# Batch 0 of a cross-attention and lookup-FFN layer: the sixteenth weight lookup moved between the two score stages

## The reference

```python
def _attn(q, k, v):
    s = jnp.einsum('bhqd,bhkd->bhqk', q, k) * SCALE
    p = jax.nn.softmax(s, axis=-1)
    return jnp.einsum('bhqk,bhkd->bhqd', p, v)
...
q = _ln((x @ Wq + bq).reshape(b, s1, H, HD), qn_w, qn_b)
k = _ln(kv[..., :HD], kn_w, kn_b)
ctx = _attn(qT, k.transpose(0, 2, 1, 3), v.transpose(0, 2, 1, 3))
ctx_dca = _attn(qT, k_dca.transpose(0, 2, 1, 3), v_dca.transpose(0, 2, 1, 3))
out = (ctx + ctx_dca) @ Wo + bo
...
def _ghost_linear(x, idx, lut):
    w = lut[idx]
    return jnp.einsum('bsh,oh->bso', x, w)
h = jax.nn.silu(gate) * up
...
x = x + _L0_xattn_ref(_layernorm(x, axis=-1), ctx_1024, ...)
x = x + _L0_ffn_ref(_layernorm(x, axis=-1), lut, gate_idx, up_idx, down_idx)
```

## Time and profile before

| | |
|---|---|
| time, median of 3 runs | 803.22 us (802.91 to 804.98) |
| the profiled execution's own time | 803.17 us |
| its span, first to last instruction | 801.4 us |
| granted TensorE clock, mean of the span | 0.985 |
| PE busy | 753.8 us |
| DVE, ACT, POOL busy | 502.3, 480.0, 279.2 us |
| batch 0's first score stage, on PE | from 54.9 us |
| batch 0's second score stage, on PE | 135.72 us to 201.82 us |

### The profile page before, as it was taken

How to read it: one execution, slowest core, us unless ns; L and a number is a source line. 1 busy time by engine, 2 the same in 40 slices (tenths; PEclk the granted TensorE clock), 3 DMA queues, 4 the chain that set the end, 5 groups by cost and what they waited for, 6 DMA issues and landing times.

```text
span 801.4 us, 14897 instructions
## 1 busy us (share of the span) xinstructions
PE 753.8 (94%) x5881; PEld 308.2 (38%) x5881; DVE 502.3 (63%) x966; ACT 480.0 (60%) x976; POOL 279.2 (35%) x283
## 2 busy tenths in 40 slices
PE   2887895999999999999999999999999999999998
PEld 1342231333443333324543332235433333265445
DVE  8979999577777994225879953228599810153221
ACT  3579887577456896662658866635489856511100
POOL 4996433002663322113843321035622310014320
PEclk9998998899999999999999999999999999999999
DMA  8639997577330001321400003223000000100001
GB/s 253 173 104 281 290 287 218 144 195 143 103 86 2 1 1 30 77 53 60 113 16 1 1 14 79 55 66 53 3 1 1 1 27 28 37 18 1 1 13 40
DMA packets 75909, 61.49 MB, mean 77 GB/s; under 512 B 34944, under 2 KB 62336, under 8 KB 75584
## 3 DMA queue, kind: packets, MB, share of 16 engines
q1 hardware_dynamic: 75056, 60.29, 28.3%
q10 hardware_dynamic: 784, 0.26, 0.2%
HBM read 43.55 MB, written 10.55 MB: 68 GB/s over the span
## 4 chain that ended last, share of the span: by engine, by line
PE 73%; DVE 13%; issue 5%; POOL 4%; ACT 3%; DMA 2%; SPq 0%; DVEq 0%; POOLq 0%
PE ps L1782 46%; PE ps L2169 8%; PE ps L2150 6%; PE ps L2121 5%; PE ps L1854 5%; POOL hrstd L745 2%; PE ps L2156 2%; DVE arena L1197 2%; ACT ps L1077 2%; DMA wf_lo<-in_idx 1%; PE ps L2017 1%; DVE stat L1258 1%; DVE arena L1338 1%; DVE nmax L1575 1%; DMA arena<-in_x 1%
## 5 line engine op out<-in xcount | busy, mean ns | idle before, releaser
L1782 PE MATMUL ps<-arena,wf_hi 128*128 128x512 f16 (+1 forms) x704 | 201.4, 370 | 0.8 <-DVE arena L1218 0.8
L1077 ACT ACTIVATE ps<-ps,nmax 128x496 f32<-128x496 f32 x256 | 166.3, 652 | 23.1 <-DVE nmax L1580 23.1
L1109 ACT ACTIVATE arena<-ps 128x1024 f32<-128x1024 f32 x128 | 124.1, 1021 | 89.1 <-PE ps L2156 89.1
L1782 PE MATMUL ps<-arena,wf_lo 128*128 128x512 f16 (+1 forms) x352 | 130.0, 369 | 0.0
L1782 PE MATMUL ps<-wf_hi,arena 128*128 128x512 f16 (+3 forms) x374 | 114.8, 368 | 0.6 <-DVE arena L1222 0.6
L745 POOL TENSOR_TENSOR hrstd<-hvar,mhalf 128x16 f32<-128x16 f32 (+1 forms) x33 | 100.2, 3049 | 43.4 <-DVE hvar L1328 43.3
L1782 PEld LDWEIGHTS ps<-arena,wf_hi 128*128 128x128 f16 x704 | 64.8, 98 | 83.7 <-issue 20.5
L1854 PE MATMUL ps<-arena,wf_lo 128*32 128x512 fp8e4 (+1 forms) x1056 | 65.9, 390 | 9.4 <-DVE wf_lo L1206 7.8
L689 POOL TENSOR_TENSOR xrstd<-xvar,mhalf 128x1 f32<-128x1 f32 x32 | 21.3, 666 | 151.9 <-DVE xvar L1263 151.9
L1782 PE MATMUL ps<-wf_lo,arena 128*128 128x512 f16 (+3 forms) x187 | 68.5, 366 | 0.0
L2169 PE MATMUL ps<-arena 128*32 128x512 f32 x512 | 68.3, 605 | 0.0
(11 more groups left out here) (164 smaller groups left out, 1073.5 us busy)
## 6 DMA issues: line engine op xcount, KB each, us to landing
arena<-bits SPq DMA_DIRECT2D x124, 128.0 KB, 3.8
arena<-in_x SPq DMA_DIRECT2D x32, 256.0 KB, 2.9
wf_lo<-in_idx SPq DMA_DIRECT2D x10, 512.0 KB, 5.1
bits<-wf_hi SPq DMA_DIRECT2D x10, 384.0 KB, 5.8
out<-arena SPq DMA_DIRECT2D x15, 256.0 KB, 2.1
wf_lo<-in_idx SPq DMA_DIRECT2D x11, 256.0 KB, 8.7
arena<-in_ctxT SPq DMA_DIRECT2D x5, 512.0 KB, 3.7
v_next<-arena SPq DMA_DIRECT2D x8, 256.0 KB, 6.3
```

What stands on the lines that cost most here:

```text
L1077: last = act.activation(sc, sc, ACT.Exp, bias=nmax[:, 0, t, h:h + 1], accum_out=den[:, 0, t, h:h + 1])
L1109: act.activation(probs[n_ % 2][:, 2 * p:2 * p + 2, :], ps[:, bank:bank + 2, :], ACT.Exp).then_inc(s["probs_set"], 1)
L1782: last = pe.matmul(dst, l, r, start=(first and i == 0), stop=(stop and i == len(todo) - 1))
```

## The change

Lookup 15 leaves slot 0 and is done on PE between the two score stages, ahead of the four transposes. Each slot's lookup on PE and its high part on ACT is then that of one chunk more: `look_up(16+n)` and `lookup_out(16+n)` in slot n. DVE's part of a slot keeps its numbers: `one_hot(17+n)`, `low_out(15+n)`; slot 15 gets the last `one_hot(32)`, which stood in batch 1's `core`. Of the two lookups at the start of batch 1 one is left (32, at AHEAD). The last early projection goes to a bank of the scores (TB) and no more stands in the list `SHARED`; it waits for the exponentials of step 29, and `scores_t(0)` waits for its result to be out. On ACT `lookup_out(14)` moves behind the exponentials of step 30, and the last `early_out` and `lookup_out(15)` stand behind the logarithm. On DVE `low_out(14)` and both halves of `one_hot(15)` stand ahead of the last row sum, one half of `one_hot(16)` behind it and the other behind `caugT`, and the four products that make the low halves of Wo, which stood behind `caugT`, go two by two into slots 0 and 1.

```diff
@@ SHARED, LATE
-    if EARLY_FROM <= i_ < EARLY_FROM + len(EARLY):
+    if EARLY_FROM <= i_ < EARLY_FROM + len(EARLY) - 1:
         SHARED += [("early", i_ - EARLY_FROM)]
...
-LATE = {AHEAD: NCH - 2, AHEAD + 1: NCH - 1}
+LATE = {AHEAD: NCH - 1}
...
+        early_bank = lambda e: TB if e == len(EARLY) - 1 else shared_bank("early", e)
@@ ACT, prepare
-                if S_ONE <= slot < S_SUM:
+                if S_ONE <= slot < S_SUM - 1:
                     for c in lookups_in(slot):
                         if 0 <= c - EARLY_FROM < len(EARLY):
                             early_out(c - EARLY_FROM)
-                        if c < NQ - 1:
+                        if c < NQ - 2:
                             lookup_out(c)
+                if slot == S_SUM - 2:
+                    lookup_out(NQ - 2)
+                if slot == S_SHIFT + 1:
+                    early_out(len(EARLY) - 1)
+                    lookup_out(NQ - 1)
                 if slot >= S_TWO:
                     for c in lookups_in(slot):
-                        lookup_out(c - 2)
+                        lookup_out(c - 1)
@@ DVE, batch 1's core
                     normalise(a, 1, False)
-                    one_hot(NCH - 1, (0,))
                     low_out(NCH - 2)
                     residual(0, prev)
                     moments(2, 0, prev, rows_of(0))
-                    one_hot(NCH - 1, (1,))
@@ DVE, prepare
+                if slot == S_SUM:
+                    low_out(NQ - 2)
+                    one_hot(NQ - 1)
+                if slot == S_SHIFT:
+                    one_hot(NQ, (0,))
                 if slot == S_SHIFT + 1:
+                    one_hot(NQ, (1,))
+                if slot in (S_TWO, S_TWO + 1):
                     dve.wait_ge(s["wo_hi"], G)
-                    for g in range(G):
+                    for g in range(slot - S_TWO, G, 2):
                         low(wo[1][:, g, :], st_o[:, g * D:(g + 1) * D], wo[0][:, g, :]).then_inc(s["wo_lo"], 1)
-                if slot == S_SUM:
-                    one_hot(NQ - 1, (1,))
                 for c in lookups_in(slot):
-                    if c < NCH - 1:
-                        one_hot(c, (0,) if c == NQ - 1 else range(NJ))
-                    if slot < S_SUM - 1 and c:
-                        low_out(c - 1)
-                    if slot >= S_SHIFT + 1:
+                    if slot < S_SUM - 1:
+                        one_hot(c)
+                        if c:
+                            low_out(c - 1)
+                    elif slot >= S_TWO:
+                        one_hot(c)
                         low_out(c - 2)
@@ PE, early, scores_t, prepare
+                if e == len(EARLY) - 1:
+                    pe.wait_ge(s["S_exp"], NS - 2)
+                else:
+                    wait_bank("early", e)
...
+                    elif prev is None:
+                        wait_early(len(EARLY) - 1)
...
+                if slot == S_SHIFT:
+                    look_up(NQ - 1)
                 for c in lookups_in(slot):
                     if slot < S_SUM and c:
                         look_up(c - 1)
                     elif slot >= S_TWO:
-                        look_up(c - 2)
+                        look_up(c - 1)
```

More of the change, by code:

```diff
@@ L903, in early_out @@
                         act.wait_ge(s["tr_lo"], len(UNITS_0))
-                    act.activation(v_early[t], ps[:, shared_bank("early", e), :], ACT.Copy, scale=1.0 / WS).then_inc(s["v_evac"], 1)
+                    act.activation(v_early[t], ps[:, early_bank(e), :], ACT.Copy, scale=1.0 / WS).then_inc(s["v_evac"], 1)
                 else:
                     act.wait_ge(s["k_done"], e - T + 1)
-                    act.activation(k_early[t], ps[:, shared_bank("early", e), :], ACT.Copy).then_inc(s["k_evac"], 1)
+                    act.activation(k_early[t], ps[:, early_bank(e), :], ACT.Copy).then_inc(s["k_evac"], 1)
             def square(a, u, first):
@@ L1083, in core @@
                     between(S_ONE + m)
+                between(S_SUM)
                 dca_exp(a, T - 1)
@@ L1894, in early @@
                 w, c_ = (wk if kind == "k" else wv), (cT_second if kind == "w" else cT_early)
-                wait_bank("early", e)
+                if e == len(EARLY) - 1:
+                    pe.wait_ge(s["S_exp"], NS - 2)
+                else:
+                    wait_bank("early", e)
                 if e == 0:
@@ L1902, in early @@
                     terms += [(sel["k"][:, :], b16[:, :])]
-                product(ps[:, shared_bank("early", e), :], terms).then_inc(s["k_done" if kind == "k" else "v_done"], 1)
+                product(ps[:, early_bank(e), :], terms).then_inc(s["k_done" if kind == "k" else "v_done"], 1)
             def wait_early(e):
```

## The result

The changed kernel takes 820.66 us (median of 4 executions, 817.91 to 822.57) against 803.07 for the kernel before (4 executions, 801.23 to 804.98): a ratio of 1.0216, 95% interval 1.0176 to 1.0256. It is slower by 17.6 us; forecast were 822.7 and a range of 812 to 828. The profiled execution is the one of 817.91 us, span 816.1, mean clock 0.987, so what its trace accounts for is 14.7 us. The work did not change: the busy times on the page differ from the earlier trace rows by 2 us or less.

A forecast was written before the change was run, and what follows sets the result against it. PE bounds the kernel, through its idle or slow stretches in batch 0. 803.2 - 0.4 (stages) + 10.8 (slot waits) - 0.2 (slot 5) + 2.3 (batch 1) + 6.0 + 1.0 (clock) = 822.7 us, range 812 to 828.

The forecast's parts named there:

- The slots' waits: Slots 4, 8 and 12: low halves wait for low_out behind attn_lo, 3.9, 3.45 and 3.45 us, together 10.8 us lost.
- The wait at batch 1: First lookup of batch 1 (32): its low half waits for low_out(31) behind two normalisations, 2.3 us lost.
- The lookup that left batch 1: Start of batch 1: one lookup fewer on PE, counted at nothing; bound a gain of 1.9 us.
- a sign of being wrong: Batch 1: its chain getting shorter with the lookup that left it was listed as showing the prediction wrong.
- The gain between the stages: Between the score stages, to scores_t(2): gain 0.4 us; bounds a gain of 1.1 and a loss of 0.5.
- as fallen: Lookup 15 between the stages: PE's clock taken as already halved, so the lookup takes 3.61 us.
- The clock in the waits: Half-speed work after the new waits: 2.0 us for each of three slot waits, 1.0 at batch 1.
- the bound below (the clock holds): Clock loss in all four new waits: lower bound 0, upper bound 10.8 us.
- Both rows that gave the price: Earlier trace: half clock after PE waits of 1.95 and 3.02 us, read as 1.9 and 2.7 us lost.
- The rival with a clock that holds: New waits bring no clock fall: 815.7 us; chance 0.18.

The follow-up runs named there:

- slot part alone: Kernel before with only DVE's slot work put one chunk back (one_hot(16+n), low_out(14+n) in slot n): 819.55 us against 803.8, ratio 1.0202.
- second profile: Profile from running the unaltered changed kernel again: median 820.76 us against 803.5 for the kernel before, ratio 1.0203.
- waits filled: Changed kernel with PE making the high half of the lookups in slots 4, 8 and 12 four times over: 816.88 us, against 820.76 for the changed kernel.
- last version: Changed kernel with DVE also one chunk on, attn_lo behind, lookup 32 behind output rows 1, low_out ahead of the masks: 796.56 us, ratio 0.9914 to before.
- transition alone: Changed kernel between the score stages, but slots as before (lookup 15+n in slot n), lookups 31 and 32 at batch 1: 799.54 us against 803.5.

## Why the prediction was right, and where its terms were off

**The slots' waits** were the main term and came out to the hundredth: 3.91, 3.45 and 3.45 against 3.9, 3.45 and 3.45, each behind the `attn_lo` that was named. The kernel with the slot part alone shows that they need nothing else of the change, and the one with `attn_lo` moved that the order on DVE is what makes them. The rule by which they could be read off the trace of before: the result that a slot waits for is ready when its chain on DVE ends, and that moment was in the trace; only the place that asks for it moved.

**A term was left out.** A lookup that is cut in two by a wait takes longer by more than the wait: slot 12, whose clock stayed at 1.00, took 7.33 us (195.20 to 202.53), that is 3.70 + 3.45 + 0.18. The term could have been read before: slot 5 took 4.10 us there, 3.70 + 0.22 + 0.18. Four such cuts make 0.7 us.

**The wait at batch 1** was 2.26 against 2.3. **The lookup that left batch 1** was counted at nothing with a bound of 1.9; from output rows 0 to the first gate matmul it is now 25.01 us (246.69 - 221.68) against 25.34 before (231.92 - 206.58), so it gave 0.33. In the second profile it is 24.46, a gain of 0.88. So batch 1's chain did get a little shorter, which the prediction had named as a sign of being wrong; the size is under 1 us.

**The gain between the stages** was put at 0.4 and is 1.9 in the profiled execution. The sum took the clock "as fallen" for lookup 15. It ran at full clock after 3.26 us of idleness, and the execution in which it did not (with lookup 32 moved, 3.60 us) prices that step at 0.95 us. From the start of lookup 15 to `scores_t(2)` even that execution took 14.8 us where the prediction has 15.3 (148.4 - 133.1). This other 0.5 is mostly in DVE's chain, whose durations were added end to end although the rows overlap a little (138.57 + 1.41 against 139.89). The chain itself was right. The clock fell later, behind the wait of 2.35 us, and that fall cost nothing: from lookup 16's low half to `scores_t(2)` it is 6.34 us (147.29 - 140.95), and just as long in the kernel with `low_out(31)` in slot 15, whose clock stayed at 1.00 and in which PE waits for `low_out(16)` instead:

```profile
141.77 1.05 PE L1868 MATMUL ps<-arena,wf_lo 128*32 128x512 fp8e4 x16 [2.36 <-DVE wf_lo L1213]
...
147.13 1.05 PE L1868 MATMUL ps<-arena,wf_lo 128*32 128x512 fp8e4 x16 [1.48 <-DVE wf_lo L1213]
148.11 0.83 PE L2169 MATMUL ps<-arena 32*128 32x512 f16 x12
```

One count ahead of the prediction needs a correction: ahead of `shift` stand one `low_out` and half a mask more than before, not one and a half masks; three halves stand there now, and two did.

**The clock in the waits** was put at 7.0 us. In the profiled execution it fell in two of the four places and cost 0.15 + 1.43 in slots 4 and 5 (`scores_t(5)` to `scores_t(6)` takes 5.13, less 3.70) and 1.64 in slot 9: 3.2 us. Filling the three waits of the slots gave back 3.9 us by the medians and 2.95 by the profiles, where I counted 6.0 for them. So both the bound below (the clock holds) and the value taken were off, and the truth lies between. Both rows that gave the price lie behind two waits and not one: the 3.02 us stands behind the 5.38, and behind the 1.95 us PE waited again in the profile of before:

```profile
60.33 1.47 PE L2121 MATMUL ps<-arena 32*128 32x512 f16 x12 [1.54 <-ACT arena L940]
```

That may be why they priced a single wait too high; no run separates it. The Trainium skill's rule in "TensorE: Matmul & The Clock Gate", section "HAM oscillation", that a long enough wait between bursts makes the next burst start at half rate, holds in these traces often but not each time: slot 12's wait brought no fall here, and in slot 8 the low half itself still ran its 1.05 us at full clock before the fall.

The sum of the profiled execution: -1.9 between the stages, +10.8 waits, -0.4 for slot 5 (4.10 us before, 3.70 without its wait), +0.5 for the cuts, +3.2 clock, +2.4 at batch 1 with its cut, -0.3 for the lookup that left, +0.4 that the first score stage ended later: 14.7, as measured. The median is 2.75 us above this execution; the executions that make it have a lower clock, and where they lost the time no trace shows. So the forecast of 822.7 lay 2.0 above the median but 4.8 above the execution that can be followed: the clock was put 3.8 too high and the gain 1.5 too low, and the cuts that were left out took some of that back. That it came as near to the median as it did is in part luck; the waits are not. The rival with a clock that holds (815.7) is refuted by the windows and by the run with the waits filled.

**Where the expected gain of the change went:** it is there, 4.0 us when the slots keep their old numbers and 7.2 us in the last version, in which all engines are shifted. The change moved PE and ACT by one chunk and left DVE where it was, and that used up the slot of slack in which DVE's chain had run out.

## What to carry to other kernels

When work in a software pipeline is moved by one step on one engine, list every result that it consumes and look up in the trace at which moment of its own step that result is ready; the slack of a whole step can hide a chain that is as long as a step. If an engine's program order puts a cheap result that others wait for behind a wait of its own, put the cheap result first. Where executions differ by as much as the change is worth, compare stretches between two events of the profile and not the totals alone. A gap that is filled on PE is worth its idle time only if the next stage does not ask an engine for the same thing earlier.

## What the runs showed of the hardware that was not expected

The same wait on PE may or may not bring the clock down. In seven profiles PE stood idle ahead of lookup 15 for 2.59 to 3.30 us, and the lookup took 2.05 us each time; in three it stood for 3.00, 3.15 and 3.50 us, and the lookup took 3.35, 3.60 and 3.54. The 3.50 and one of the seven, 2.88, are two executions of the same kernel. The wait of 3.45 us in slot 12 brought a fall in the run with the slot part alone and none in the two profiles of the changed kernel; that of 2.26 us at batch 1 brought one in the run with the waits filled, at a moment when the changed kernel had none. What a fall costs differs too: 1.4 to 1.7 us behind the waits of slots 4, 8 and 12, 2.8 in slot 1 of the kernel with the transition alone, and nothing in slot 1 of the changed kernel, where DVE's chain took as long as PE did at half clock. What decides whether the clock falls is open, and no run here was made to tell it. For a forecast of this kernel, a wait of some 3.5 us is priced at its length plus 1.0 to 1.3 us, an estimate: the third part of the 2.95 and 3.9 us that filling three of them gave back.
